# Step 0 of the first stage runs through to its router before step 1's scores; all keys of step 1 ahead of the router's transposes; two weight loads one step later

## The reference

```python
h = _L0_tok_ref(x, conv_w, conv_b, pos_table)             # patches @ conv_w + position
h = jnp.concatenate([h, txt], axis=1)                     # 16 x 113 x 192
h = h + _L0_attn_ref(_layernorm(h), memory, Wq, ...)      # one head, keys and values also from 8 memory rows
h = h + _L0_ffn_ref(_layernorm(h), scale, gate_w, ...)    # top 4 of 16 experts
h = h + _L1_attn_ref(_layernorm(h), ...)
h = h + _L1_ffn_ref(_layernorm(h), ...)
# inside _L0_ffn_ref
t = xf * jax.lax.rsqrt(jnp.mean(xf * xf, -1) + EPS) * scale
g = t @ gate_w.T + gate_b
vals, idx = jax.lax.top_k(g, 4)
w = softmax(vals) / 4
h = _swiglu(t @ w1[e] + b1[e]);  y = h @ w2[e] + b2[e]    # for the chosen experts e
```

## Time and profile before

| what | us |
|---|---|
| three timed runs | 963.55, 969.58, 977.57 (median 969.58) |
| the profiled execution | 964.52 |
| its span, first to last instruction | 962.8 |
| TensorE busy | 796.4 (83%) |
| VectorE busy | 500.0 (52%) |
| ScalarE busy | 305.6 (32%) |
| GpSimd busy | 367.0 (38%) |
| GpSimd's scatters, 64 in all | 152.4 |
| mean granted TensorE clock | 0.884 of full speed |

### The profile page before, as it was taken

The page is one execution under the profiler, slowest core; times in us unless marked ns, Lnnn a source line. Parts: engine busy times, 40 slices in busy tenths (PEclk is TensorE's granted clock), DMA queues, the critical chain, the costliest instruction groups (busy, mean ns, idle before and its releaser), DMA issues.

```text
span 962.8 us, 14910 instructions
## 1 busy us (share of the span) xinstructions
PE 796.4 (83%) x4888; PEld 563.7 (59%) x4888; DVE 500.0 (52%) x1247; ACT 305.6 (32%) x571; POOL 367.0 (38%) x237
## 2 busy tenths in 40 slices
PE   7998962699889999988979787878889889888572
PEld 4665751367667777756757574564646646656251
DVE  4465553436444444748676965274754754724220
ACT  1122321123233333323423337234442352342100
POOL 3018888787810487678786100010010010000000
PEclk9999865789999999987979898857999999999795
DMA  8831114345542344352111000000000000000000
GB/s 237 256 100 51 37 28 87 75 94 117 110 119 84 87 116 120 97 160 60 34 29 31 1 2 1 1 1 1 1 1 1 14 1 0 14 1 2 14 1 15
DMA packets 81396, 52.96 MB, mean 55 GB/s; under 512 B 42942, under 2 KB 76719, under 8 KB 80305
## 3 DMA queue, kind: packets, MB, share of 16 engines
q1 hardware_dynamic: 27042, 29.63, 10.9%
q0 software_dynamic: 40960, 11.98, 6.9%
q10 hardware_dynamic: 13328, 10.49, 3.8%
HBM read 29.53 MB, written 21.69 MB: 53 GB/s over the span
## 4 chain that ended last, share of the span: by engine, by line
PE 63%; POOL 12%; DVE 11%; issue 6%; ACT 3%; DMA 2%; DVEq 0%; ACTq 0%; SPq 0%; POOLq 0%
PE ex_up L1161 7%; PE ex_up L1162 6%; POOL work L230 6%; POOL xs_scratch L219 5%; PE ps L2300 4%; PE ex_yp L1184 3%; PE ex_yp L1185 3%; PE ps L2231 3%; PE ps L1382 3%; PE ps L1384 2%; PE ps L1383 2%; PE ps L1377 2%; PE ps L2240 2%; PE a_ps L399 1%; PE ps L1393 1%
## 5 line engine op out<-in xcount | busy, mean ns | idle before, releaser
L230 POOL DMA_INDIRECT work<-ys_scratch,place x64 | 153.3, 2395 | 86.5 <-DMA ys_scratch<-ex_yb 56.3
L219 POOL DMA_INDIRECT xs_scratch<-e_t,e_routed x64 | 152.4, 2381 | 42.3 <-issue 29.6
L1161 PE MATMUL ex_up<-e_wa,ex_x 128*128 x176 | 75.8, 513 | 11.2 <-issue 7.2
L1268 DVE TENSOR_SCALAR ex_bb<-ex_up 128x384 f32<-128x384 f32 x44 | 24.8, 563 | 115.1 <-PE ex_up L1162 99.2
L1162 PE MATMUL ex_up<-e_wb,e_ex_x 65*128 x176 | 74.2, 503 | 0.0
L2488 POOL TENSOR_SCALAR f_veps<-f_mv 113x4 f32<-113x4 f32 x12 | 2.3, 193 | 176.4 <-DVE f_mv L2551 176.4
L1223 ACT ACTIVATE ex_sg<-ex_up 128x384 f32<-128x384 f32 x44 | 21.6, 490 | 110.3 <-PE ex_up L1162 110.3
L1162 PEld LDWEIGHTS ex_up<-e_wb,e_ex_x 65*128 65x128 f32 x176 | 34.8, 198 | 24.9 <-issue 2.7
L1161 PEld LDWEIGHTS ex_up<-e_wa,ex_x 128*128 128x128 f32 x176 | 30.6, 193 | 28.8 <-issue 16.0
L2436 ACT ACTIVATE f_pT<-ps 113x452 f32<-113x452 f32 x48 | 26.2, 546 | 66.7 <-PE ps L2240 66.6
L2510 POOL TENSOR_TENSOR H<-H,f_hh 113x768 f32 (+1 forms) x4 | 7.2, 1809 | 101.7 <-DVE f_hh L2654 101.7
(11 more groups left out here) (376 smaller groups left out, 1933.1 us busy)
## 6 DMA issues: line engine op xcount, KB each, us to landing
ys_scratch<-ex_yb ACTq DMA_DIRECT2D x44, 192.0 KB, 5.1
ex_xb<-xs_scratch SPq DMA_DIRECT2D x86, 96.0 KB, 5.1
xs_scratch<-e_zeros SPq DMA_DIRECT2D x62, 96.0 KB, 4.9
e_wa<-in_wa SPq DMA_DIRECT2D x4, 1152.0 KB
e_wb<-in_wb SPq DMA_DIRECT2D x4, 576.0 KB
e_wa<-in_patches SPq DMA_DIRECT2D x4, 432.0 KB, 9.5
out<-H SPq DMA_DIRECT2D x4, 339.0 KB
w4a<-in_w4a SPq DMA_DIRECT2D x1, 1216.0 KB
```

What stands on the lines that cost most here:

```text
L219: nc.gpsimd.indirect_dma_start(out=dram.xs, out_offset=bass.IndirectOffsetOnAxis(ap=S.pos[:, j, k:k + 1], axis=0), in_=S.t[:, j, :], in_of ...
L230: nc.gpsimd.indirect_dma_start(out=S.yk[:, it % 2, j, k, :], out_offset=None, in_=dram.ys[it // X.steps], in_offset=bass.IndirectOffsetOnA ...
L1161: mm(o, x1[:, p % 3, t], S.wa[:, bass.ds(w, 2 * I)], start=True, stop=False)
```

## The change

In step 0, TensorE no longer ends with qk(1) and attended, projected of step 0. It does attended(0), Q1 of step 1, projected(0), then Q2, K1 and K2 of step 1, one warm-up, t_transposed(0) and logits(0). Step 1 is then scores(1), the first half of values(1), ranks(0), the second half, transposed(2), p_transposed(1), qk(2), attended(1), projected(1). Steps 2 and 3 are as before. The warm-ups after p_transposed(0) and in step 1 are gone. `qk` takes the tiles it is to do, `values` the half, and `qk_copy` is split in `q_copy` and `k_copy`. ScalarE and VectorE follow the same order. On VectorE, positions(0) moves up behind softmax_in(1), ahead of norm1(2), and mean1(2) into step 0. GpSimd's list has eight and eight scatters of step 0 in place of five and eleven. `later_loads` moves from step 1 to step 2. No computation is dropped or added.

```diff
@@ TensorE
             def body(it, first, last):
...
-                values(it)
-                if not first:
+                values(it, 0)
+                if it == 1:
+                    ranks(0)
+                values(it, 1)
+                if it > 1:
                     t_transposed(it - 1)
-                if it == 1:
-
-                    pe.wait_ge(*att.free(it, PT))
-                    warm(nc, S, att.bank(PT), 1)
                 if not last:
                     transposed(it + 1, proj, X1, xn, xn_ok)
                 p_transposed(it)
-                if not first:
+                if it > 1:
                     logits(it - 1)
-                if it == 1:
-                    warm(nc, S, rout.bank(RK), 3)
-                    ranks(0)
                 if first:
-                    warm(nc, S, att.bank(O1), 1)
+                    attended(0)
+                    qk(1, Q1)
+                    projected(0)
+                    qk(1, Q2, K1, K2)
+                    warm(nc, S, rout.bank(T1), 1)
+                    t_transposed(0)
+                    logits(0)
+                    return
                 if not last:
-                    qk(it + 1)
+                    qk(it + 1, Q1, Q2, K1, K2)
                 attended(it)
@@ ScalarE
             def body(it, first, last):
                 exp(it)
-                if not first:
+                if it > 1:
                     rows_out(it - 1)
                 v_copy(it)
-                if not first:
+                if it > 1:
                     t_copy(it - 1)
                 if not last:
                     x_high(it + 1)
                 p_copy(it)
-                if it == 1:
+                if first:
+                    o_copy(0)
+                    q_copy(1)
+                    rows_out(0)
+                    k_copy(1)
+                    t_copy(0)
+                    keep(0)
+                    return
+                if it == 2:
                     later_loads()
                 if not last:
-                    qk_copy(it + 1)
-                if not first:
+                    q_copy(it + 1)
+                    k_copy(it + 1)
+                if it > 1:
                     keep(it - 1)
                 o_copy(it)
@@ GpSimd
-            scatter(0, 0, 5)
+            scatter(0, 0, 8)
             root2(1)
             root1(3)
-            scatter(0, 5, 16)
+            scatter(0, 8, 16)
@@ VectorE
             def body(it, first, last):
-                if not first:
+                if it > 1:
                     mean2(it - 1)
-                if not last:
+                if not (last or it == 1):
                     mean1(it + 1)
                 softmax_in(it)
-                if not first:
+                if it == 1:
+                    positions(0)
+                if it > 1:
                     rows_out(it - 1)
                 if not last:
                     norm1(it + 1)
                 v_copy(it)
                 softmax_out(it)
-                if not first:
+                if it > 1:
                     t_copy(it - 1)
                 if not last:
                     x_low(it + 1)
-                if not first:
+                if it > 1:
                     top4(it - 1)
                     chosen(it - 1)
-                if it == 1:
-                    positions(0)
+                if first:
+                    o_copy(0)
+                    residual(0)
+                    mean2(0)
+                    q_copy(1)
+                    mean1(2)
+                    k_copy(1)
+                    rows_out(0)
+                    t_copy(0)
+                    top4(0)
+                    chosen(0)
+                    return
                 if not last:
-                    qk_copy(it + 1)
+                    q_copy(it + 1)
+                    k_copy(it + 1)
                 o_copy(it)
```

More of the change, by code:

```diff
@@ L412, in transposed, with qk @@
                     i.then_inc(tiles.filled.sem, 1)
-            def qk(it):
+            def qk(it, *tiles):
                 pe.wait_ge(*proj.copied(it, X1))
                 pe.wait_ge(*proj.copied(it, X2))
[L418 to L441, removed]
+                for n in tiles:
+                    col = w.q if n < K1 else w.k
+                    c0, c1 = (0, LO) if n in (Q1, K1) else (LO, D)
+                    pe.wait_ge(*proj.free(it, n))
+                    o = images(proj.bank(n)[0:c1 - c0, 0:G * NK])
+                    ws = slice(col + c0, col + c1)
+                    mm(o, S.w1h[:, ws], c1h[:], start=True, stop=False)
+                    mm(o, S.w1h[:, ws], c1l[:], start=False, stop=False)
+                    mm(o, S.w1l[:, ws], c1h[:], start=False, stop=False)
+                    mm(o, S.w2hh[:, ws], c2s[:], start=False, stop=False)
+                    mm(o, S.w2l[:, ws], c2s[0:HI, :, :], start=False, stop=True).then_inc(proj.filled.sem, 1)
@@ new lines, in values @@
+            def values(it, h):
+                pe.wait_ge(*proj.free(it, V0 + h))
+                for j in (2 * h, 2 * h + 1):
+                    o = proj.bank(V0 + h)[0:NK, (j % 2) * D:(j % 2 + 1) * D]
+                    ws = slice(w.v, w.v + D)
+                    mm(o, c1h[:, j, :], S.w1h[:, ws], start=True, stop=False)
+                    mm(o, c1l[:, j, :], S.w1h[:, ws], start=False, stop=False)
+                    mm(o, c1h[:, j, :], S.w1l[:, ws], start=False, stop=False)
+                    mm(o, c2s[:, j, :], S.w2hh[:, ws], start=False, stop=False)
+                    m = mm(o, c2s[0:HI, j, :], S.w2l[:, ws], start=False, stop=True)
+                m.then_inc(proj.filled.sem, 1)
@@ L514, in lead @@
                 pe.wait_ge(rest_ok, 5)
-                qk(0)
+                qk(0, Q1, Q2, K1, K2)
                 pe.wait_ge(S.consts_ok, S.n_consts)
@@ L619, in keep, with q_copy @@
                     cp(h, h, ACT.Identity, scale=up1[:, j:j + 1], bias=nm[:, 0, j:j + 1]).then_inc(hx_ok.sem, 1)
-            def qk_copy(it):
+            def q_copy(it):
                 act.wait_ge(*done(proj.filled, it, Q1))
@@ L625, in qk_copy, with k_copy @@
                 cp(q1[:], images(proj.bank(Q1)[0:LO, 0:G * NK])[:, :, 0:N], ACT.Identity, bias=S.c0a[:, w.cq:w.cq + 1]).then_inc(proj.out(Q1), 1)
+            def k_copy(it):
                 act.wait_ge(*done(proj.filled, it, K2))
@@ L669, in lead @@
                 x_high(0)
-                qk_copy(0)
+                q_copy(0)
+                k_copy(0)
             def body(it, first, last):
                 exp(it)
-                if not first:
+                if it > 1:
                     rows_out(it - 1)
                 v_copy(it)
-                if not first:
+                if it > 1:
                     t_copy(it - 1)
```

## The result

The changed kernel takes 980.42 us (median of 19 runs, 970.21 to 989.79), the kernel before 965.15 us (19 runs, 957.66 to 977.57). The ratio is 1.0157 [1.0127, 1.0186]: some 15 us slower, under the 2% that I called a difference, but well outside the range of 957.5 to 972.5. I had forecast -2.4 us. The profiled execution has a span of 977.3 us, against 962.8.

What follows compares the result with a forecast made beforehand. The prediction took GpSimd's scatters (37% of 60 to 185 us) as the bound. Of 4.4 us gained at #1, 0.7 is left at root2(2); with the shorter stop before #18, -2.4: 967.05 - 2.4 = 964.6 us, range 957.5 to 972.5.

Steps and rivals of the forecast that it cites:

- Weight loads later: w1w and w1g on ScalarE, moved from step 1 to step 2: nothing taken, with 0.8 us of cover.
- A late landing: Rival: scatter #16 lands after 12.2 us, #18 starts +1.4 us, sum -1.0; chance 0.20 together with "nothing arrives".
- #18 waits for #16: GpSimd's stop before scatter #18 is for the landing of #16; it shrinks from 2.05 to 0.30 us.
- ScalarE's hold: w1g's issue holds ScalarE's queue 6.50 us, q_copy(3) about 106.5; K2 needs it about 107.3, so no cost.
- #1 at 70.2: GpSimd's first scatter of step 0 starts at 70.2 us against 74.64, range 66.8 to 72, one slow stretch of 1.7 counted.
- Slower: Rival: without warm-ups TensorE's clock stays at half from 43.7 until past scatter #1; +2.7 us with three stretches more; chance 0.15.
- attended(0) at half clock, 3.7 us: TensorE, step 0: attended(0)'s 16 matmuls run at half clock, 3.7 us, ending at 47.45.
- root2(1) at 92.35, after 0.8 of waiting: GpSimd, behind eight scatters: could start at 91.55, waits 0.8 us for mean2(1), which ends at 92.35.
- root2(2) at 121.25 after a hole of 2.7: GpSimd, step 2: reaches root2(2) at 118.55, idles 2.7 us, starts at 121.25 against 121.97.
- 28.9 us as before: Step 2's chain from root2(1) to root2(2) takes 28.9 us, as from 88.03 to 116.94 in the kernel before.
- The sum: Whole change: scatter #18 starts at 127.35 against 129.79, everything behind only moves; -2.4 us.
- The experts' stage: Sign of being wrong: the experts' stage itself changes its length, where it was expected only to move.

Runs made afterwards that it cites:

- b_split: The kernel before with the load of w1w cut in two (96 partitions and the 97th); ratio 1.0038 [0.9988, 1.0088].
- b_split2: The kernel before with both weight loads moved to step 2 and w1w cut in two; ratio 1.0018 [0.9978, 1.0057].
- b_loads2: The kernel before with only the two weight loads moved from step 1 to step 2, w1w whole; ratio 1.0169 [1.0110, 1.0228].
- a_split: The changed kernel with w1w's load cut in two (96 partitions and the 97th), loads still in step 2; ratio 1.0042 [1.0003, 1.0081].
- a_swap: The changed kernel with w1g issued first and w1w, whole, behind it; ratio 1.0133 [1.0064, 1.0201].
- a_warm: The changed kernel with w1w cut in two (96 partitions and the 97th) and five warm-ups put back; ratio 1.0001 [0.9959, 1.0044].
- a_half: The changed kernel with w1w's load cut at row 48, into 48 and 49 partitions; ratio 1.0049 [1.0000, 1.0097].
- a_late: The changed kernel with the two loads issued, whole, in step 3 in place of step 2; ratio 1.0099 [1.0070, 1.0128].
- a_again: The changed kernel unaltered, for a second profile; span 972.6 us.

## Why the prediction was wrong

**The step that failed** is "Weight loads later", where I wrote "I take nothing", with the rival "A late landing" as its only price. The mechanism was there in both halves (one engine's worth of DMA, and #18 waiting for #16); the size was not. I bounded #16's landing by the slowest row, 12.2 us, and got +1.4. It measured 21.0, so the stop was 8.62 in place of 0.30. The slowest row was no bound: it was #5, the last ahead of root2(1), issued at 85.59 and landed at 97.8, when w1w was all but through (its last packets run in 98 to 100 us). Without w1w whole under it #5 took 9.0 to 10.3 us (b_split, b_split2, b_loads2). In the new place w1w runs until 136, 19 us behind #16's issue. Had I asked which scatter the 12.2 belonged to, the trace would have said that the last of a batch is the one to look at, and that the 7.7 of the others says nothing. A landing near the load's end, 136, would have been the nearer estimate, though b_loads2 shows that it is only that. In the whole time this step is some 11 of the 15 us (a_split; b_loads2 against b_split2 gives 15, from three runs of the first).

**The rest, point by point.**
- *#18 waits for #16*: right. Wherever there is a stop and the trace has the landing, #18 starts 0.6 to 0.8 us behind #16's landing, or #34 behind #32's.
- *ScalarE's hold*: I wrote 6.50 us with 0.8 of cover. It was 7.98, and q_copy(3) came at 112.16, 3 us behind its group. TensorE, at half clock, ran through qk(3) without a hole even so (106.47 to 115.9), so K2 was not held up, and a_swap shows no gain from freeing the queue.
- *#1 at 70.2*: it came at 71.98, at the far end of the range (66.8 to 72). I took one slow stretch of 1.7 us; the clock was at half from 60.4 to 80.8. a_warm puts the warm-ups at 3.6 us of #1 (71.98 to 68.39), but a_half, with the changed kernel's instructions up to there, has #1 at 70.14, so single profiles don't tell 2 us. The Trainium skill, "TensorE: Matmul & The Clock Gate", "What's actually happening", which I named in my rival *Slower*, has the throttled clock as the default, released by activity. By that rule the trace agrees only in part: the clock fell to half with TensorE busy in all of 60 to 72, and #1 was still not later than before.
- *attended(0) at half clock, 3.7 us*: right, 3.73.
- *root2(1) at 92.35, after 0.8 of waiting*: 93.36, without waiting. The 1.4 us that I added for norm1(2) beside scatters did not come (its four rows took 1.28 in all, at 71.58).
- *root2(2) at 121.25 after a hole of 2.7*: 124.15 after 4.93. Its cause is a step of mine, "28.9 us as before": it took 30.8. The clock was at half from 97.9 to 114.9, where before it was back by about 105. The same stretch took 28.9 in a_split and a_late, 30.9 in a_half and 35.4 in a_again, so it moves by itself from one execution to the next, as the clock does (0.56 on average over a_again's stretch), and is no property of the order that I could show.
- *The sum*: without the load, -2.4 was forecast, and a_split measures +0.4% (0.0 to +0.8%), about +4 us: also wrong in sign, if by less. Its root2(1) stood at 98.22, that of the changed kernel at 93.36, with the same instructions up to there; it goes with the clock, on average 0.57 against 0.72 in 60 to 100 us. Which part of the sum cost these 4 us stays open.
- *The experts' stage*: a sign of being wrong that I named was that it changes its length. It did in the first profile (227.9 for 234.4 us), but not in a_again (234.9).
- *The chances*: 0.98 for within 2% held, but the slower rival I named was the clock. The one that decided I had valued at a gain of 1.0 us.

## What to carry to other kernels

Before a load is moved, see how many DMA engines it takes (its share of 16 in a window of its own) and whose landing it then lies under; here 97 partitions put a large load on one engine, and one row cut off spread it. Read the slowest landing with its place: where transfers share a semaphore, look at the last one of a batch, since the others looked on time here and a good median said nothing. And an order that gains 5 us at one stage's end is worth little until the intervals of the whole show it.

## What the runs showed that I had not expected

- A scatter of 8 us took 21.0 us beside a transfer that used a sixteenth of the DMA (6.0% of the engines' time), and in a_late #32 and #33 took 15.8 and 16.0 us although they were issued 6 us and more behind the load's end.
- The issue of a small load behind a one-engine load holds its queue: w1g took 6.50 to 11.23 us to issue behind w1w whole, 0.32 behind w1w cut, and 0.34 ahead of it.
- The clock fell to half while TensorE counted as busy without a hole (60 to 72 us), and came back at different times with the same instructions: root2(1) stood at 91.5, 93.4, 93.6, 98.0 and 98.2 us in five profiles (a_half, changed, a_again, a_late, a_split) whose instructions up to there are the same.
- GpSimd stops once in sixteen scatters, until the one two places back has landed: before #18, #34 and #50, for 2.05, 3.75 and 5.38 us in the kernel before. Of the late landings here only those of #16 and #32 stopped it.
